# Decoder layer with a mixture of experts: tokens scattered to fixed expert regions in four router batches, and results scattered back to token rows

## What is computed

```
h = x + attention(rms_norm(x, norm1_w), Wq, Wk, Wv, Wo)
...
logits = x @ router_w + router_b
topv, topi = jax.lax.top_k(logits, TOP_K)
topw = jax.nn.softmax(topv, axis=-1)
...
h1 = jnp.einsum('bsd,edf->ebsf', x, W1) + b1[:, None, None, :]
h2 = jnp.einsum('bsd,edf->ebsf', x, W2) + b2[:, None, None, :]
h = h2 * jax.nn.silu(h1)
eo = jnp.einsum('ebsf,efd->ebsd', h, W3) + b3[:, None, None, :]
return jnp.einsum('bse,ebsd->bsd', comb, eo)
```

## Time and profile before

| | |
|---|---|
| median of 3 runs | 283.98 us (283.62 to 284.4) |
| the profiled execution: its time | 283.89 us |
| its span, first to last instruction | 282.1 us |
| PE busy | 219.0 us (78%) |
| DVE busy | 193.5 us (69%) |
| ACT busy | 119.1 us (42%) |
| POOL busy | 109.7 us (39%) |
| mean granted clock of PE | 0.887 |

### The profile page before, as it was taken

How to read it: one execution, slowest core, us unless ns; L and a number is a source line. 1 busy time by engine, 2 the same in 40 slices (tenths; PEclk the granted TensorE clock), 3 DMA queues, 4 the chain that set the end, 5 groups by cost and what they waited for, 6 DMA issues and landing times.

```text
span 282.1 us, 6021 instructions
## 1 busy us (share of the span) xinstructions
PE 219.0 (78%) x1736; PEld 195.2 (69%) x1737; DVE 193.5 (69%) x526; ACT 119.1 (42%) x393; POOL 109.7 (39%) x188
## 2 busy tenths in 40 slices
PE   0489999999999999997999752299999999940000
PEld 0368999899899887886998552188999999930000
DVE  7034799887799999997776348736767676733434
ACT  1436666567566654446654202043434434410000
POOL 0242235444555455442322240353553422017771
PEclk9999999999999999799999655579999999985555
DMA  7799700000008000000000000011211233011112
GB/s 239 171 364 344 167 3 0 2 0 3 2 3 224 0 2 3 1 0 12 9 13 19 19 12 0 20 29 31 70 51 47 44 48 39 19 37 47 55 47 74
DMA packets 21335, 16.00 MB, mean 57 GB/s; under 512 B 3033, under 2 KB 18465, under 8 KB 21313
## 3 DMA queue, kind: packets, MB, share of 16 engines
q1 hardware_dynamic: 19248, 12.02, 14.7%
q0 software_dynamic: 1344, 2.76, 4.8%
q10 hardware_dynamic: 720, 0.95, 1.0%
HBM read 11.78 MB, written 3.93 MB: 56 GB/s over the span
## 4 chain that ended last, share of the span: by engine, by line
PE 62%; DVE 16%; POOL 6%; issue 6%; DMA 4%; ACT 2%; SPq 2%; POOLq 0%; DVEq 0%; ACTq 0%
PE bank L665 12%; PE bank L559 11%; PE bank L481 9%; PE bank L676 7%; PE bank L533 7%; POOL yg L470 4%; DVE smax L872 3%; PE bank L569 3%; PE bank L529 3%; PE bank L576 2%; PE bank L517 2%; DVE x L924 2%; DMA bias_col<-in_L_xattn_bv 2%; PE bank L518 1%; PE bank L519 1%
## 5 line engine op out<-in xcount | busy, mean ns | idle before, releaser
L559 PE MATMUL bank<-vbd,pt_sb 128*128 128x34 f32 x384 | 46.3, 276 | 0.2 <-ACT pt_sb L755 0.2
L559 PEld LDWEIGHTS bank<-vbd,pt_sb 128*128 128x128 f32 x384 | 44.8, 192 | 0.3 <-ACT pt_sb L755 0.3
L458 POOL DMA_INDIRECT early<-xm_scratch,tok_i x26 | 25.8, 994 | 45.3 <-DMA early<-xm_scratch,tok_i 27.8
L872 DVE TENSOR_REDUCE smax<-bank 128x8 f32<-128x512 f32 x48 | 32.6, 679 | 13.3 <-PE bank L533 13.3
L665 PE MATMUL bank<-xgt,w_now 128*128 128x128 f32 x320 | 40.4, 281 | 0.4 <-ACT xgt L827 0.4
L665 PEld LDWEIGHTS bank<-xgt,w_now 128*128 128x128 f32 x320 | 38.7, 198 | 0.8 <-ACT xgt L827 0.8
L380 POOL TENSOR_TENSOR k<-kt,cst 128x512 f32<-128x512 f32 x24 | 25.2, 1052 | 33.1 <-ACT kt L745 33.1
L880 DVE TENSOR_TENSOR s_sb<-bank,smax 128x512 f32<-128x512 f32 x48 | 33.2, 691 | 2.1 <-PE bank L481 0.3
L831 ACT ACTIVATE s_sb<-bank,w_now 128x128 f32<-128x128 f32 x80 | 22.8, 368 | 23.8 <-PE bank L665 23.8
L533 PE MATMUL bank<-k,q 64*128 64x256 f32 x192 | 28.8, 411 | 0.0
L1092 DVE SCALAR_TENSOR_TENSOR pt_sb<-bank,w_now,s_sb 128x128 f32<-128x128 f32 x80 | 22.5, 343 | 7.3 <-ACT s_sb L831 6.6
(11 more groups left out here) (159 smaller groups left out, 345.4 us busy)
## 6 DMA issues: line engine op xcount, KB each, us to landing
w_up<-in_L_ffn_W SPq DMA_DIRECT2D x2, 2048.0 KB, 12.3
w<-in_L_ffn_W SPq DMA_DIRECT2D x8, 256.0 KB, 6.3
y_scratch<-eo SPq DMA_DIRECT2D x1, 1536.0 KB, 6.9
y_scratch<-eo SPq DMA_DIRECT2D x10, 128.0 KB
cst<-in_consts ACTq DMA_DIRECT2D x1, 672.5 KB, 4.0
early<-in_x SPq DMA_DIRECT2D x1, 512.0 KB, 5.9
early<-in_ctx SPq DMA_DIRECT2D x1, 512.0 KB, 4.2
xm_scratch<-xm SPq DMA_DIRECT2D x8, 64.0 KB, 1.5
```

The lines of the kernel that those rows point to most:

```text
L458: pool.indirect_dma_start(xg[:, j, :], None, xm_d[:, :], bass.IndirectOffsetOnAxis(ap=tok_i[:, j:j + 1], axis=0)).then_inc(g_gather, 16)
L559: k = mm(ps_o[:, c:c + 34], pt_sb[:, h, (2 * b + jj) * P:(2 * b + jj + 1) * P], vbd[:, i, b, j, :, :].rearrange("k p c -> k (p c)"), start ...
L872: v.tensor_reduce(smax[:, b, :], ps_score[b][:, :].rearrange("q (p k) -> q p k", k=S), AX.X, ALU.max).then_inc(d_mx, 1)
```

## The change

Router batches. The 8 token tiles are routed in four batches, (0, 1, 2), (3, 4), (5, 6) and (7). For each, PE turns and makes logits (`route_turn`, `route_logits`), DVE picks the two largest with the instructions for the 8 largest values and their indices (`top_two`), PE ranks (`rank`), and DVE computes slots (`slots`). The first two batches stand inside the last attention steps, 22 to 25.

Fixed regions. Each expert has a region of 9 tiles of rows in DRAM, one array `slot_rows` for a token's first and one for its second expert, cleared at the start from `blank`. `finish` writes each token twice (`xm2`), each copy with a 129th number that names its result row. POOL scatters both copies to their slots (`to_slots`, two indirect DMAs for each token tile). A tile is read with plain loads, its two arrays added by DVE (`take`); the sum gives the tokens and the row numbers.

Static tiles. After the first batch the first tile of each of the experts 0 to 3 is closed: later tokens of these experts go to the next tile. The four closed tiles are loaded (`xs_a`) and run in fixed code. The rest, listed by `tile_list`, runs in the loop as before, loaded pair by pair by SP.

Results. POOL scatters each finished tile from `eo` to token rows in `y_rows` (`send_out`), one DMA in flight at a time; `keep_out` waits for these. The last stage reads its rows with four plain loads.

```diff
...
+            def send_out(u, rows):
+                pool.indirect_dma_start(y_d[:, :], bass.IndirectOffsetOnAxis(ap=idx_c[u][:, :], axis=0),
+                                        rows[:, u, :], None).then_inc(y_sent, 16)
+
+            def pause(n):
+
+                if not isinstance(n, int) or n >= 1:
+                    pool.wait_ge(g_idle, n)
+                g.tensor_tensor(idle[:, :], half_neg[:, :], half_neg[:, :], ALU.mult).then_inc(g_idle, 1)
+
+            def next_ids(p):
+                pool.wait_ge(d_id, p + 1)
+                if not isinstance(p, int) or p >= 1:
+                    pool.wait_ge(g_idm, p)
+                g.tensor_tensor(id_n[:, :], id_f[:, :], ones2[:, :], ALU.mult).then_inc(g_idn, 1)
...
+            def send_pair(p, rows):
+                for u in range(2):
+                    pool.wait_ge(g_idm, p + 1)
+                    if not isinstance(p, int) or p > 0 or u > 0:
+                        pool.wait_ge(y_sent, p * 32 + 16 * u)
+                    pause(p * 4 + 2 * u)
+                    g.tensor_copy(idx_c[u][:, :], id_m[:, u:u + 1]).then_inc(g_idc, 1)
+                    pool.wait_ge(g_idc, p * 2 + u + 1)
+                    pool.wait_ge(d_eo, p * 2 + u + 1)
+                    pause(p * 4 + 2 * u + 1)
+                    send_out(u, rows)
...
+            def to_slots(t):
+
+                for b, ts in enumerate(BATCHES):
+                    if t == ts[0]:
+                        pool.wait_ge(d_slot, b + 1)
+                if t == 0:
+                    pool.wait_ge(pre_done, 32)
+                    pool.wait_ge(c_id, 1)
+                if t == NS:
+                    pool.wait_ge(in_xa, 32)
+                for k in range(2):
+                    if t >= 1:
+                        pool.wait_ge(g_slot[k], 16 * t)
+                    pool.indirect_dma_start(xs_d[k][:, :], bass.IndirectOffsetOnAxis(ap=slot_i[:, k, t:t + 1], axis=0),
+                                            xm2[:, t, k, :], None).then_inc(g_slot[k], 16)
...
+            g.memset(blank[:, :], 0.0).then_inc(c_pre, 1)
...
+                if it == STEPS - 1:
+                    to_slots(0)
+                if it == STEPS:
+                    to_slots(1)
+                    to_slots(2)
+                if it == STEPS + 1:
+                    to_slots(3)
+                if it == STEPS + 2:
+                    next_ids(0)
+                    keep_ids(0)
+            for t in range(NS + 1, NT - 1):
+                to_slots(t)
+            next_ids(1)
+            to_slots(NT - 1)
+
+            send_pair(0, eo_a[:, 0:2, :])
+            keep_ids(1)
+            next_ids(2)
+            send_pair(1, eo_a[:, 2:4, :])
...
+            with pool.Fori(0, last + 1) as i:
+                keep_ids(i + PA)
+                next_ids(i + PA + 1)
+                send_pair(i + PA, eo)
...
+            def take(src, p):
+
+                if isinstance(p, int):
+                    if p < PA:
+                        dve.wait_ge(in_xa, 32)
+                    if p >= 1:
+                        dve.wait_ge(pe_xgt, p)
+                        dve.wait_ge(g_idn, p)
+                else:
+                    dve.wait_ge(pe_xgt, p)
+                    dve.wait_ge(g_idn, p)
+                v.tensor_tensor(xs[:, :, :], src[:, 0], src[:, 1], ALU.add).then_inc(d_xs, 1)
...
+                dve.wait_ge(pe_e, 2 * i + 2 * PA + 2)
+                dve.wait_ge(y_sent, 32 * i + 32 * PA)
+                keep_out(1)
```

More of the change, by code:

```diff
@@ L166, in decoder_kernel @@
-        tok_i = sb("tok_i", [P, NG], I32)
-        xs = sb("xs", [P, 2, P])
+        blank = sb("blank", [P, FILL * ROW])
+        xs_a = sb("xs_a", [P, 2, NA, ROW])
+        xs_b = sb("xs_b", [P, 2, 2, ROW])
+        xs = sb("xs", [P, 2, ROW])
+        spare = sb("spare", [P, 2])
+        id_f = sb("id_f", [P, 2])
+        id_n = sb("id_n", [P, 2])
+        id_m = sb("id_m", [P, 2])
+        ones2 = sb("ones2", [P, 2])
+        idle = sb("idle", [P, 1])
+        idx_c = [sb(f"idx_c{u}", [P, 1], I32) for u in range(2)]
@@ L189, in decoder_kernel @@
         in_brow = sem("in_brow")
+        in_xa = sem("in_xa")
+        in_xs = [sem(f"in_xs{u}") for u in range(2)]
+        in_y = [sem(f"in_y{c}") for c in range(4)]
         out_done = sem("out_done")
@@ L264, in decoder_kernel @@
         d_fin = sem("d_fin")
-        xm_d = nc.dram_tensor("xm_scratch", (NT * P, D), F32, kind="Internal").ap()
-        y_d = nc.dram_tensor("y_scratch", (NJ * P, D), F32, kind="Internal").ap()
+        xs_d = [nc.dram_tensor(f"slot_rows{k}", (SLOT_TILES * P, ROW), F32, kind="Internal").ap() for k in range(2)]
+        y_d = nc.dram_tensor("y_rows", (2 * NT * P + P, D), F32, kind="Internal").ap()
+        slot_tiles = [x.rearrange("(a q) e -> q a e", q=P) for x in xs_d]
         block = ctx.enter_context(nc.Block())
@@ L975, in _ @@
                     minus_max(it, 1)
+                if it == STEPS - 2:
+                    top_two(0)
+                if it == STEPS - 1:
+                    slots(0)
+                if it == STEPS:
+                    top_two(1)
+                if it == STEPS + 1:
+                    slots(1)
+                if it == STEPS + 2:
+                    take(xs_a[:, :, 0:2, :], 0)
                 if it >= 3:
                     finish(it - 3)
-            chain = [0]
-            def link(ins):
-                chain[0] += 1
-                ins.then_inc(d_rt, 1)
-                dve.wait_ge(d_rt, chain[0])
@@ L1087, in pair_of, with inner @@
                 return dve.snap(w & 7), dve.snap((w >> 3) & 7)
-            def hidden(u, done):
+            def inner(u, w, done):
                 for c in range(4):
@@ new lines, in _ @@
+                dve.wait_ge(pe_h, 4 * i + 4 * PA + 8)
+                inner(1, w_now[:, 1, :], 8 * i + 8 * PA + 12)
+                dve.wait_ge(d_hh, 8 * i + 8 * PA + 16)
+                load_up(1, eb)
+                dve.wait_ge(pe_e, 2 * i + 2 * PA + 3)
+                dve.wait_ge(y_sent, 32 * i + 32 * PA + 16)
+                keep_out(0)
+            dve.wait_ge(pe_e, 2 * last + 2 * PA + 2)
+            dve.wait_ge(y_sent, 32 * last + 32 * PA)
+            keep_out(1)
+            v.tensor_tensor(gate_v[:, 0, :], top_v[:, :, 1], top_v[:, :, 0], ALU.subtract).then_inc(d_gate, 1)
```

719 lines of the change are left out of this document (430 added, 289 removed).

## The result

The changed kernel takes 294.76 us (median of 4 runs, 292.96 to 296.29), the kernel before 283.99 (4 runs, 283.62 to 284.4). The ratio is 1.0381, with a 95% interval of 1.0342 to 1.0419. It is slower by 3.8%. The profiled execution took 293.39 us, of which 291.5 is the span. Executions more than 1.5% above the fastest of their kernel are left out of all ratios; among the kernels of the experiments this takes three of six from shifted, the profiled one among them, and none from the others.

The account below looks back on a forecast made before the run. Four stages, each with its own limit, PE's in the expert stage; after the change POOL's sends. 199.8 to the sends, 75.0 for them and 19.3 of tail gave 294.1 us of span, 296 us in all; range 283 to 306.

Parts of the forecast that it names:

- Start-up: POOL clears `blank` before its third key expansion, bounded at 5.6 us; 4.9 us of slack; put at 0, at worst 1 us.
- End of attention: Steps 22 to 25: routing waits make the last `h` 8 us late and the last `xm` 175.9 in place of 162.4.
- The one-for-one price of the start: Routing before the experts: a last `xm` 7 us earlier would bring the time from 296 to 289.
- The rival for a faster routing: Routing is hidden better than figured, last `xm` at 168.9; 289, or 277 with sends under 3.2 us; chance 0.12.
- Static tiles and tile list: After the last `xm`: `slots(3)` at 188, `tile_list` done at 194, POOL starts sending from 199.8.
- The sends: POOL's result scatters, one closed chain per tile: 3.75 us (3.35 to 4.05) against PE's 3.2; 20 tiles, 75.0 us.
- The 2.15 for a landing: Skill's estimate for landing a 64 KB scatter, giving a 3.4 us tile and a time of 289; 2.5 was taken.
- Then the time is at or under 284: Outcome if scatters land in 2 us or under, PE has no gaps after 200, or a dynamic tile starts before 195.
- PE keeps the pace: Expert loop: with sends of 3.2 us or less the loop is as before, 283.6 us, no change; chance 0.06.
- Tail: From the last landing to the end: four plain loads, eight tiles, norms and store, 19.3 us where it was 31.7.
- The range: Whole time: 285 to 306 us from landing, routing start and final load; low end taken to 283.
- PE at the lower clock: Expert loop: waits drop PE's clock for good, 5.6 us a tile, time 325; chance 0.12 for all above 303.

Follow-up runs that it names:

- shifted: The changed kernel with the first routing batch's top_two, slots, rank and sends each one attention step later: 298.69 us.
- more_pause: The changed kernel with two more pause operations on POOL for each tile, between the landing of the scatter before and the index cast: 307.26 us.
- two_arrays: The changed kernel with even and odd tiles' results scattered to two arrays; final loads read only the first, half the results left out: 290.48 us.
- two_sum: two_arrays with both arrays loaded at the end and added, nothing left out: 294.35 us.
- two_banks: two_arrays with a pair's down-projections in two PSUM banks and PE's wait for keep_out(1) removed; half the results left out: 283.45 us.
- banks: The changed kernel, one result array, with a pair's down-projections in two PSUM banks and PE's wait for keep_out(1) removed: 299.15 us.
- one_port: The changed kernel with DVE's copy of the up-weights written as a scalar_tensor_tensor of the same values: 298.91 us.
- banks_act: banks with the loop's copy of the up-weights made by ScalarE in place of DVE: 292.18 us.
- banks_port: banks with DVE's copy of the up-weights written as a scalar_tensor_tensor of the same values: 300.24 us.
- late3: The changed kernel with the scatters of token tile 3 moved behind POOL's row_scale(23), one step later: 294.21 us.
- all_port: The changed kernel with two_sum's arrays, two_banks' banks, late3's move and the up-weights copy as a scalar_tensor_tensor on DVE: 292.73 us.

## Why the prediction was right, point by point

The forecast was 296.0 us and slower; it is 294.76. In the span, 294.1 was summed and 291.5 measured. By the sum the third send would have gone at 201.05 (199.8 and the 1.25 us ahead of an issue) and went at 197.98: 3.1 us less. From there to the last landing 73.75 were summed and 75.8 measured: 2.05 more. The tail took 1.6 less. So the path is the one that was forecast, and that the number is off by only 1.2 us owes something to luck, as errors of 3.1 and 2.05 us have opposite signs.

**Start-up: right.** Summed at 0. Clearing `blank` took 2.14 us, where the bound was 5.6, and the scores behind the third key expansion begin at 27.50 (27.22 before).

**End of attention: right.** Step 23 at 152.2 (151.6), last `h` 168.7 (168.85), load landed 172 (170.4), POOL free for `row_scale(23)` 174.5 (173.6), last `xm` written 175.9 (175.15). What I had not foreseen is PE's granted clock. In this execution PE waits 1.11 us for `h` in step 23; its granted clock over 150 to 160 is 0.68 of the full 2.4 GHz in the mean, and the same 16 passes of `values` that took 1.97 us in the earlier trace rows took 3.63:

```profile
153.81 3.63 PE L683 MATMUL bank<-vbd,pt_sb 128*128 128x34 f32 x16 [0.20 <-ACT pt_sb L952]
```

Its last `values` began at 160.58 where I had 159.6. The sum absorbed that because the load came 1.6 us earlier. The fall at this place does not belong to the change: in more_pause, two_arrays, two_sum, two_banks, banks and one_port, which are alike up to there, the same passes took 1.97 us (in banks_act and banks_port 3.57 and 3.63), and the last `h` came no later than 169.04.

**The one-for-one price of the start: too high.** The rival for a faster routing had put a price of 7 us on 7 us at the last `xm`. late3 moved the last `xm` by 3.6 and the time by 0.5. PE's first `up` moved by 0.5 only, since it comes behind the load of the static tiles and not behind the last `xm`, and with the chain of sends behind it nothing of that reached the last send.

**Static tiles and tile list: summed 3 to 4 us too late.** `slots(3)` ended at 184.1, not 188: single operations were closer (starts 0.2 to 0.22 us apart for the small ones where I took 0.25), and PE's clock was at its full level from 180 (1.00). The first static send went at 190.74.

**The sends: right, with errors that cancel.** I summed 3.75 us a tile; 3.80 were measured in the mean. Landing took 2.4 to 2.5 us in the median, as in the gathers of the earlier trace rows. The small operations overlap (starts 0.13 us apart) where I took 0.08 between them, and the gap ahead of the issue is 0.46 us where I took 0.27. With nothing held a tile is 3.6, so the sum was 0.15 too high for what it counted. The lock, which brings 0.11 a tile here and 0.40 in banks, and the slow first landings were not in it at all. The 2.15 for a landing, the prediction's estimate from the Trainium skill (DMA: Bandwidth & Descriptors, Anatomy of one DMA), would have made it 289; the trace shows 2.3 at the least and 2.4 in the median. Of the lock, the Trainium skill (SBUF — State Buffer, SBUF: two separate sides) says that VectorE and GpSimd share a pair of ports as an exclusive lock, for VectorE's two-port modes and, against a GpSimd operation that reads SBUF, for two SBUF inputs. The runs agree: a pause of 0.70 us under the COPY in banks, a send of 2.00 under the form with two SBUF inputs in one_port, and 0.20 and 1.01 in the mean in the loop of banks_act, where DVE makes neither form of the copy.

**"Then the time is at or under 284" if PE keeps pace: only half the story.** The rival "PE keeps the pace" took for granted that behind the sends stands PE at 3.2 us a tile. two_arrays showed 3.6 there, because both halves of a pair shared a bank; only with two banks did it come to 283.45, where that rival had 283.6. The change brought that shared bank, and I gave it no price.

**Tail: 17.7 us for 19.3.** First load 2.7 (SP's issue at 273.78, first use at 276.49) for 3.0; a token tile 1.17 us with its norm's part for 1.28 and 0.04.

**The range: not what its parts give.** 296 with -8, +6, 4 either way and +3 is 284 to 309 when added up, not 285 to 306. The measured time lies well inside either.

**PE at the lower clock: did not happen in the loop.** The granted clock is 1.00 (2.4 GHz) in each window from 210 to 260 with PE busy 7.9 to 9.3 of 10 us. It did fall at the end of attention, above. The oscillation that the Trainium skill tells of (TensorE: Matmul & The Clock Gate, HAM oscillation) did not show in this loop.

## What to carry to other kernels

A scatter that must wait for the one before it cost 2.4 us of landing here plus everything that POOL does in between; as soon as this exceeds what the engines need for a tile, it is the kernel's pace, and busy shares don't show it. Before opening such a chain, look for the bound right behind it: here that was a saved PSUM bank. Two arrays alone gained 0.4 us with nothing left out, late3 0.5, two banks alone lost 4.4, and all together gained 9.0. If an engine that issues DMAs is on the path, look at its shortest operation: one that takes 0.70 us in some rounds and 0.19 in others is being held by another engine, and the timeline of the two side by side names it.

## What the runs showed that I had not expected

A VectorE operation on 128x1032 float32 from SBUF to SBUF held up the POOL operation that began under it, in both forms that were tried, for the rest of its duration (0.51 us of 0.70; sends that end 0.89 us after a copy of 1.23). The shorter `xs<-xs_b` (128x258, 0.43 us, two inputs in SBUF) did so too: a `pause` at 221.64 in the changed kernel took 0.48 us under it. An operation with a PSUM source did not: pauses of 0.19 us lie under `pt_sb<-bank` of 1.13 us.

What happens when the copy begins inside a send depends on its form, in every run alike. The COPY that begins 0.28 to 0.54 us into a send prolongs it until 0.12 us after its own end: the seven in banks that begin 0.47 us in all make sends of 1.29 or 1.30 us. One that begins 0.56 to 0.78 us in waits itself, and ends 0.5 us after the send. POOL's and DVE's timelines in the changed kernel:

```profile
230.63 1.01 POOL L492 DMA_INDIRECT y_rows<-eo,idx_c  x1 [0.45 <-issue]
```

```profile
231.24 0.90 DVE L1326 COPY w_now<-w_up 128x1032 f32 x1 [0.22 <-DVE pt_sb L1335]
```

The other form, with two inputs in SBUF, never did either when it began 0.47 us or more into a send: in banks_port, one_port and all_port all these sends took 1.01 us. That fits with all_port, which has no long send, and with one_port, which has one in each pair.

How strongly a closed loop depends on where such a meeting falls was new to me as well: with the same work, banks settled into a round in which both meetings recur in nearly every pair, and lost 4.4 us by a change that only gave PE a second bank and removed a wait.
